# One-head cross-attention: queries from two fp16 parts, and rows turned by a SyncE transfer

## The chip, the cores and the metric

The kernel runs on one core of one Trainium2 chip. The metric is the device time of one execution in microseconds (us); the median of the runs shown is compared, lower is better.

## What is computed

A decoder of two layers on 2048 rows of width 256, with a context of 1601 rows of width 192. Layer 0: self-attention with 16 heads, cross-attention with 16 heads, a mixture of 8 experts (top 2). Layer 1: linear attention with a short convolution, **cross-attention with one head**, and a product quantised to fp8. The change is in the one-head cross-attention, whose reference is, on layer-normed rows:

```python
query = image_features @ Wq + bq
key = text_features @ Wk + bk
value = text_features @ Wv + bv
scores = query @ key.T / sqrt(256)
weights = softmax(scores, axis=-1)
attended = weights @ value            # added to the rows x
```

## The kernel before, in words

`cross_one_head` (L2338 to L2706) works on 16 tiles of 128 rows (T = 16). The two weight matrices Wq and Wk are folded into one matrix `fold` before the stage, so that a query of 192 (padded to 256) columns meets the context itself; `near` is its bias, `side` the share of the bias in a row's sum. Each engine has its own instruction stream, written out by hand; semaphores order them. For tile n:

- GpSimd (L2384 to L2394) normalises the rows into `oxn` (L2390) and multiplies them by `side` into `oprods` (L2394). L2390 of tile n waits until TensorE has turned tile n-2, L2394 until VectorE has summed the previous product.
- TensorE turns the rows in two transposes (`turn_x`, L2421) into the bank `ops_x`; ScalarE copies them to `oxt` (`copy_x`, L2524); TensorE makes the query with four fp32 products against `fold` (`query`, L2428; the trace shows two instructions for each). ScalarE evicts it with its bias as the high fp16 part `oqh` (L2531), VectorE makes the low part `oql` (L2598).
- `score`: each of four blocks of up to 512 keys gets five fp16 products (L2441 to L2445) into the four banks `ops_s`.
- VectorE takes the maximum of the first 1024 keys (`front`, L2609) and of the other 577 (`maximum`, L2614), and makes the bias `onm` of the exponential (L2621). ScalarE takes the exponentials of both parts into `opn` with their sums (`weights`, L2539).
- ScalarE casts them to fp16 as the high part `oph` (`high`, L2546, in two pieces), VectorE makes the low part `opl` (`low`, L2627, in two pieces). SyncE turns each with one transposing transfer (L2405, L2409).
- `values`: 13 blocks of three fp16 products (L2459 to L2461) against the context rows into the bank `ops_o`. The other half of this bank takes the turned attention (`turn_o`, L2470) and its product with Wv (`project`, L2476), which VectorE adds to the rows (`add`, L2642). `values(n)` waits for `add(n-1)` (semaphore "o"). In between ScalarE scales and evicts the attention (`evict`, L2553) and copies it turned (`copy_o`, L2559).

The tiles overlap. In its iteration n TensorE does: score(n+1) block 0, turn_x(n+2), turn_o(n-2), score(n+1) block 1, project(n-2), score(n+1) blocks 2 and 3, query(n+2), values(n-1). ScalarE: evict(n-2), high(n, 0), copy_x(n+2), copy_o(n-2), high(n, 1), query(n+2), weights(n+1). VectorE: low(n, 0), low(n, 1), front(n+1), add(n-2), maximum(n+1), low part of query(n+2), share(n) (the reciprocal of the sum), extremes(n-2), row_sum(n+3), and for n of 1 to 7 one step on the weights of the last stage. Before its loop TensorE does score(0), turn_x(1), query(1) and ten idle products that only keep it busy (`unused`, L113); VectorE does row_sum(0), row_sum(1), front(0), maximum(0), row_sum(2), and the low part of query(1). Tile 0's query is made in the stage before.

## Time and profile before

| | us |
|---|---|
| median of 3 runs | 1683.11 |
| lowest, highest | 1682.45, 1684.7 |
| the profiled execution, its own time | 1681.9 |
| its span, first to last instruction | 1680.1 |
| busy: TensorE (PE) | 1596.0 (95%) |
| busy: VectorE (DVE) | 1503.1 (89%) |
| busy: ScalarE (ACT) | 1318.8 (78%) |
| busy: GpSimd (POOL) | 395.6 (24%) |
| mean granted TensorE clock | 0.993 of 2.4 GHz |

The profile shows one execution. PEld is TensorE's loading of weights, which runs beside its products; SPq is SyncE's queue, whose rows show the issue of a transfer. A row of the timeline gives start and duration of one instruction (or of several of one line, with their count), and in brackets how long its engine had been idle and what released it. Products are pipelined: each shows some 0.2 us more than its distance to the next. The stage of the change runs from about 1488 to 1646 us of the span.

### The profile page before, as it was taken

What the parts mean: (1) busy time and instruction counts of PE and PEld (TensorE: products, weight loads), DVE (VectorE), ACT (ScalarE), POOL (GpSimd) and SP (SyncE); (2) the same over time, 40 slices, a digit from 0 to 9 for tenths busy, and PEclk for the clock granted to TensorE, in tenths of its full rate; (3) what the DMA queues carried; (4) which work ended last, traced back from release to release, by engine and by line L of the source; (5) the groups of instructions that cost most, each with busy time, mean ns of one, the idle gap of its engine ahead of it and who ended that gap; (6) DMA issues with size and microseconds to landing.
All of it is one profiled execution on the core that took longest, in us unless ns stands there. A gap on an engine that the chain in (4) does not pass through costs nothing. (4 is left out here: it accounts for less than half of the span.)

```text
span 1680.1 us, 36592 instructions
## 1 busy us (share of the span) xinstructions
PE 1596.0 (95%) x14452; PEld 631.1 (38%) x14452; DVE 1503.1 (89%) x2190; ACT 1318.8 (78%) x2590; POOL 395.6 (24%) x658
## 2 busy tenths in 40 slices
PE   6999999999999999999999999999989999789997
PEld 3542222232223232223322222222235555657773
DVE  6899999989999999989899999999948887788867
ACT  4619999879898989898899999999985565545644
POOL 5800010212123312312211111111013443533300
PEclk9999999999999999999999999999999999999998
DMA  4001001001101200111221011010001000025551
GB/s 147 14 7 20 14 14 14 14 14 26 27 14 24 42 14 14 33 20 24 70 55 26 14 21 20 14 27 14 14 30 60 1 1 1 1 37 96 94 103 51
DMA packets 148027, 52.34 MB, mean 31 GB/s; under 512 B 137424, under 2 KB 146128, under 8 KB 147600
## 3 DMA queue, kind: packets, MB, share of 16 engines
q1 hardware_dynamic: 147152, 48.62, 14.1%
q8 instruction: 115, 1.88, 0.5%
q10 hardware_dynamic: 704, 1.38, 0.2%
q14 instruction: 56, 0.46, 0.1%
HBM read 14.07 MB, written 2.10 MB: 10 GB/s over the span
## 5 line engine op out<-in xcount | busy, mean ns | idle before, releaser
L968 DVE TENSOR_REDUCE mxp<-ps_m 128x2 f32<-128x1024 f32 (+2 forms) x928 | 1048.8, 1195 | 41.5 <-PE ps_m L747 40.1
L897 ACT ACTIVATE work<-ps_s 128x512 f32<-128x512 f32 x1856 | 1001.7, 598 | 76.5 <-PE ps_s L771 48.9
L797 PE MATMUL ps_av<-work,vst 128*32 128x256 f32 x7424 | 592.8, 391 | 14.7 <-ACT avs L904 12.3
L771 PE MATMUL ps_s<-qb,k_stack 50*128 50x512 f16 x1856 | 565.8, 382 | 0.5 <-ACT v_rows L915 0.3
L747 PE MATMUL ps_m<-k_stack,qa 48*128 48x512 f16 (+1 forms) x2048 | 534.5, 358 | 2.3 <-PEq L1123 0.5
L797 PEld LDWEIGHTS ps_av<-work,vst 128*32 128x32 f32 x7424 | 147.1, 108 | 383.1 <-ACT work L897 321.6
L771 PEld LDWEIGHTS ps_s<-qb,k_stack 50*128 50x128 f16 x1856 | 119.6, 94 | 378.6 <-ACT work L897 322.9
L747 PEld LDWEIGHTS ps_m<-k_stack,qa 48*128 48x128 f16 x2048 | 108.3, 93 | 21.5 <-DVE mxp L968 14.8
L616 POOL TENSOR_SCALAR mtmp<-negm 128x16 f32<-128x16 f32 x32 | 8.2, 255 | 390.3 <-DVE negm L973 390.2
L602 POOL COPY vst<-v_rows 128x1024 f32<-128x1024 f32 (+1 forms) x32 | 30.6, 956 | 144.4 <-PE ps_av L797 144.3
L682 POOL TENSOR_TENSOR q_rows<-avs,rc 128x256 f32<-128x256 f32 x31 | 19.2, 619 | 173.2 <-DVE rc L979 173.2
L1603 PE MATMUL pbank<-k_stack,pxh 128*128 128x512 f16 x128 | 48.7, 380 | 5.8 <-ACT pscaled L1752 3.3
L2627 DVE TENSOR_TENSOR opl<-opn,oph 128x1024 f16<-128x1024 f32 (+1 forms) x32 | 32.2, 1041 | 21.9 <-ACT oph L2546 17.7
L2459 PE MATMUL ops_o<-k_stack,opht 128*128 128x192 f16 (+1 forms) x195 | 48.0, 246 | 1.7 <-DVE x_res L2642 1.7
L1604 PE MATMUL pbank<-k_stack,pxh 128*128 128x512 f16 x128 | 48.5, 379 | 0.0
L2461 PE MATMUL ops_o<-k_stack,oplt 128*128 128x192 f16 (+1 forms) x195 | 47.9, 246 | 0.0
L2460 PE MATMUL ops_o<-rows_l,opht 128*128 128x192 f16 (+1 forms) x195 | 47.9, 246 | 0.0
L1106 POOL CAST qnat<-q_rows 128x256 f16<-128x256 f32 x60 | 22.2, 398 | 97.9 <-issue 51.2
L2531 ACT ACTIVATE oqh<-ops_x,near 128x128 f16<-128x128 f32 x30 | 9.4, 364 | 42.4 <-PE ops_x L2428 42.4
L1607 PE MATMUL pbank<-k_stack,pxl 128*128 128x512 f16 x128 | 38.1, 379 | 0.0
L1752 ACT ACTIVATE pscaled<-pbank,pmix 128x256 f32<-128x256 f32 x64 | 26.6, 465 | 13.7 <-PE pbank L1607 7.0
L2539 ACT ACTIVATE opn<-ops_s,onm 128x1024 f32<-128x1024 f32 (+1 forms) x32 | 29.4, 924 | 9.8 <-DVE onm L2621 9.5
(442 smaller groups left out, 1993.6 us busy)
## 6 DMA issues: line engine op xcount, KB each, us to landing
x_res<-in_x SPq DMA_DIRECT2D x4, 512.0 KB, 8.1
w_experts<-in_w_experts SPq DMA_DIRECT2D x1, 2048.0 KB, 8.1
out<-x_res SPq DMA_DIRECT2D x8, 256.0 KB, 2.1
v_rows<-in_ctx_c SPq DMA_DIRECT2D x1, 1664.0 KB, 7.1
work<-in_ctx_t SPq DMA_DIRECT2D x1, 1456.0 KB, 15.3
ctx_n<-in_ctx_n SPq DMA_DIRECT2D x1, 1248.0 KB, 7.6
w_qkv<-in_w_qkv ACTq DMA_DIRECT2D x1, 768.0 KB, 8.5
w_qkv<-in_w_qkv SPq DMA_DIRECT2D x1, 768.0 KB, 4.2
```

The costliest lines, as they stand in the source:

```text
L747: m = pe.matmul(ps_m[:, b, e, col:col + width], qa[n % 3][e * HALF:e * HALF + MAXROWS, a, j, :], STACKS[g][e * HALF:e * HALF + MAXROWS, gr ...
L771: pe.matmul(ps_s[:, bank, :], STACKS[part(n)][rows, group(n) * PAIRS + j, t * P:t * P + P], qb[n % 2][rows, :, j, :], start=True, stop=Tru ...
L797: m = pe.matmul(ps_av[32 * h:32 * h + 32, cols], vst[n % 2][:, t, h, :], pbuf[(tau[n] + t) % 2][:, h, cols], start=(t == 0 and half == 0), ...
L897: a.activation(pbuf[g % 2][:, h, :], ps_s[:, b, :], ACT.Exp, scale=factor).then_inc(s["exp"], 1)
L968: v.tensor_reduce(dst, src, AX.X, ALU.max).then_inc(s["mred"], 1)
L1603: pe.matmul(bank[i % 2][:, :], xh[n % 2][:, k, :], weh[:, k, cols], start=(k == 0), stop=False)
L1604: pe.matmul(bank[i % 2][:, :], xh[n % 2][:, k, :], wel[:, k, cols], start=False, stop=False)
L1607: m = pe.matmul(bank[i % 2][:, :], xl[n % 2][:, k, :], weh[:, k, cols], start=False, stop=(k == 1))
L2459: pe.matmul(att(n), pht[n % 2][0:r, t, :], vh[0:r, t, :], start=(t == 0), stop=False)
L2460: pe.matmul(att(n), pht[n % 2][0:r, t, :], vl[0:r, t, :], start=False, stop=False)
L2461: m = pe.matmul(att(n), plt[n % 2][0:r, t, :], vh[0:r, t, :], start=False, stop=(t == TM - 1))
L2627: v.tensor_tensor(pl[:, PIECES[k]], pn[n % 2][:, PIECES[k]], ph[:, PIECES[k]], ALU.subtract).then_inc(s["pl"], 1)
```

## The change

The rows and the folded weights are split into two fp16 parts each, and the query is the sum of three products of parts (high-high, high-low, low-high) in place of the fp32 product, twelve fp16 products per tile in place of four fp32 ones. The rows' parts (`xs`, 128 x 512 in fp16) are turned by one transposing transfer on SyncE's queue in place of TensorE's two transposes and ScalarE's copy. ScalarE makes the high part of the rows (`high_row`) and, once, of the weights (`fs`); GpSimd makes the low parts (`low_row`, and once for the weights). The order of GpSimd's work and the places of the new steps are in the diff. The sequence of VectorE is unchanged.

```diff
--- before.py
+++ after.py
@@ -2339,7 +2339,7 @@
 
 
     nc = prog["nc"]
-    s = {k: fresh(prog, "x" + k) for k in ("norm", "var", "root", "rstd", "xn", "xtr", "xcp", "qm", "qh", "ql", "sc", "mx", "nm", "ex", "ph", "pl", "hi", "lo",
+    s = {k: fresh(prog, "x" + k) for k in ("norm", "var", "root", "rstd", "xn", "xh", "xl", "x_in", "fp", "qm", "qh", "ql", "sc", "mx", "nm", "ex", "ph", "pl", "hi", "lo",
                                            "av", "o", "o2", "r", "rr", "oe", "otr", "ocp", "y", "pad", "sh", "neg", "sca", "top", "wf")}
     FRONT = 1024
     LAST = M - (TM - 1) * P
@@ -2349,7 +2349,9 @@
     with ExitStack() as cx:
         def sb(name, shape, dt=F32):
             return cx.enter_context(nc.sbuf_tensor(name, shape, dt))
-        xn, xt = [first[0], sb("oxn1", [P, D])], [first[1], sb("oxt1", [P, 2, P])]
+        xn = [first[0], sb("oxn1", [P, D])]
+        xs, xt = ([sb(f"o{k}{p}", [P, *shape], F16) for p in range(2)] for k, shape in (("xs", (2, D)), ("xturned", (4, P))))
+        fs = sb("ofs", [P, 2, 2, D], F16)
         qh, ql = ([first[i], sb(f"o{k}1", [P, 2, P], F16)] for i, k in ((2, "qh"), (3, "ql")))
         pn = [sb(f"opn{p}", [P, MP]) for p in range(2)]
         ph, pl = (sb(f"o{k}", [P, MP], F16) for k in ("ph", "pl"))
@@ -2381,9 +2383,13 @@
                 g.memset(oc[p][:, C + 1:D], 0.0).then_inc(s["pad"], 1)
             for rows in (ph, pl):
                 g.memset(rows[:, M:MP], 0.0).then_inc(s["pad"], 1)
+            def low_row(n):
+                g.wait_ge(s["xh"], n)
+                g.tensor_tensor(xs[n % 2][:, 1, :], xn[n % 2][:, :], xs[n % 2][:, 0, :], ALU.subtract).then_inc(s["xl"], 1)
+
             for n in range(T):
-                if n >= 2:
-                    g.wait_ge(s["xtr"], n - 1)
+                if n >= 3:
+                    g.wait_ge(s["xl"], n - 2)
                 if n == FIRST_T:
                     g.wait_ge(s["rstd"], 1)
                 if n > 0:
@@ -2392,11 +2398,28 @@
                 g.wait_ge(s["xn"], n + 1)
                 g.wait_ge(s["r"], 2 * n)
                 g.tensor_tensor(prods[:, :], xn[n % 2][:, :], side[:, 0:D], ALU.mult).then_inc(s["r"], 1)
+                if n == 0:
+                    g.wait_ge(s["fp"], 1)
+                    g.tensor_tensor(fs[:, 1, :, :], fold[:, :, :], fs[:, 0, :, :], ALU.subtract).then_inc(s["fp"], 1)
+                if n > 0:
+                    low_row(n)
 
         @block.sync
         def _(e):
+            def turn_x(n):
+                e.wait_ge(s["xh"], n)
+                e.wait_ge(s["xl"], n)
+                if n >= 3:
+                    e.wait_ge(s["qm"], n - 1)
+                if n > 1:
+                    e.wait_ge(s["x_in"], 16 * (n - 1))
+                e.dma_start_transpose(xt[n % 2][:, :, :], xs[n % 2][:, :, :].rearrange("p s d -> p (s d)")).then_inc(s["x_in"], 16)
+
+            turn_x(1)
             e.wait_ge(s["pad"], 7)
             for n in range(T):
+                if n + 2 < T:
+                    turn_x(n + 2)
                 e.wait_ge(s["ph"], 2 * n + 2)
                 if n > 0:
                     e.wait_ge(s["hi"], 16 * n)
@@ -2413,20 +2436,16 @@
 
         @block.tensor
         def _(pe):
-            def turn_x(n):
-                pe.wait_ge(s["xn"], n + 1)
-                if n > 0:
-                    pe.wait_ge(s["ql"], n)
-                for k in range(2):
-                    m = pe.transpose(ps_x[:, k, :], xn[n % 2][:, k * P:k * P + P], ident[:, :])
-                m.then_inc(s["xtr"], 1)
-
             def query(n):
-                pe.wait_ge(s["xcp"], n + 1)
+                pe.wait_ge(s["x_in"], 16 * n)
+                pe.wait_ge(s["ql"], n)
+                if n == 1:
+                    pe.wait_ge(s["fp"], 2)
                 for c in range(2):
                     for k in range(2):
-                        m = pe.matmul(ps_x[:, 2 + c, :], fold[:, k, c * P:c * P + P], xt[n % 2][:, k, :],
-                                      start=(k == 0), stop=(k == 1))
+                        for i, j in ((0, 0), (0, 1), (1, 0)):
+                            m = pe.matmul(ps_x[:, 2 + c, :], fs[:, i, k, c * P:c * P + P], xt[n % 2][:, 2 * j + k, :],
+                                          start=((k, i, j) == (0, 0, 0)), stop=((k, i, j) == (1, 1, 0)))
                 m.then_inc(s["qm"], 1)
 
             def score(n, b):
@@ -2479,18 +2498,14 @@
             def unused(count):
                 idle_products(pe, ps_i[:, :], kh[:, 0, 0:P], kh[:, 0, 0:512], count)
 
-            pe.sem_inc(s["xtr"], 1)
             pe.sem_inc(s["qm"], 1)
             for b in range(4):
                 score(0, b)
-            turn_x(1)
             query(1)
             unused(10)
             for n in range(T):
                 if n + 1 < T:
                     score(n + 1, 0)
-                if n + 2 < T:
-                    turn_x(n + 2)
                 if n >= 2:
                     turn_o(n - 2)
                 if n + 1 < T:
@@ -2519,9 +2534,11 @@
             back = a.alloc_register("one_undo")
             a.reg_load(back, undo[0:1, 0:1].bitcast(I32))
 
-            def copy_x(n):
-                a.wait_ge(s["xtr"], n + 1)
-                a.copy(xt[n % 2][:, :, :], ps_x[:, 0:2, :]).then_inc(s["xcp"], 1)
+            def high_row(n):
+                a.wait_ge(s["xn"], n + 1)
+                if n >= 3:
+                    a.wait_ge(s["x_in"], 16 * (n - 2))
+                a.copy(xs[n % 2][:, 0, :], xn[n % 2][:, :]).then_inc(s["xh"], 1)
 
             def query(n):
                 a.wait_ge(s["qm"], n + 1)
@@ -2558,24 +2575,25 @@
                     a.wait_ge(s["y"], n)
                 a.copy(oct[:, :, :], att_t).then_inc(s["ocp"], 1)
 
-            a.sem_inc(s["xcp"], 1)
             a.sem_inc(s["qh"], 2)
+            a.copy(fs[:, 0, :, :], fold[:, :, :]).then_inc(s["fp"], 1)
             a.wait_ge(s["var"], 1)
             a.activation(tmp[:, 0, FIRST_T:T], tmp[:, 1, FIRST_T:T], ACT.Sqrt).then_inc(s["root"], 1)
             a.wait_ge(s["pad"], 7)
             a.activation(warm[:, :], warm[:, :], ACT.Exp)
-            copy_x(1)
+            high_row(1)
             weights(0)
+            high_row(2)
             query(1)
             for n in range(T):
                 if n >= 2:
                     evict(n - 2)
                 high(n, 0)
-                if n + 2 < T:
-                    copy_x(n + 2)
                 if n >= 2:
                     copy_o(n - 2)
                 high(n, 1)
+                if n + 3 < T:
+                    high_row(n + 3)
                 if n + 2 < T:
                     query(n + 2)
                 if n + 1 < T:
```

## Rows read from the trace of the kernel before

**Rows 1.** Busy time: stretch, us; PE, PEld, DVE, ACT, POOL (count); clock, DMA share, GB/s

```profile
1541.09:1550.00 8.91, 8.91 (x77) 7.03 (x75) 7.62 (x19) 5.07 (x12) 3.03 (x3) 1.00 0.52 98
1621.08:1629.70 8.62, 6.87 (x60) 5.14 (x58) 6.21 (x16) 4.17 (x9) 0.00 (x0) 1.00 0.53 99
```

**Rows 2.** Timeline, middle tile: start us, us, engine, line, operation

```profile
1541.02 2.26 POOL L2390 TENSOR_SCALAR oxn<-x_res,ln_mean,ln_rstd 128x256 f32<-128x256 f32 x1 [0.46 <-PE ops_x L2421]
1541.09 2.13 DVE L2627 TENSOR_TENSOR opl<-opn,oph 128x1024 f16<-128x1024 f32 x2 [1.12 <-issue]
...
1543.78 1.91 SPq L2409 DMA_TRANSPOSE oplt<-opl  x1
...
1544.14 1.14 PE L2428 MATMUL ops_x<-oxt,fold 128*128 128x128 f32 x8
...
1544.58 0.41 DVE L2642 TENSOR_TENSOR x_res<-ops_o,x_res 128x256 f32<-128x256 f32 x1
...
1545.14 0.24 PE L2459 MATMUL ops_o<-k_stack,opht 128*128 128x192 f16 x1
...
1548.56 0.42 ACT L2553 ACTIVATE ooc<-ops_o,orr 128x192 f32<-128x192 f32 x1 [0.38 <-PE ops_o L2461]
...
1549.44 0.38 PE L2421 MATMUL ops_x<-ident,oxn 128*128 128x128 f32 x2
...
1549.66 0.38 PE L2470 MATMUL ops_o<-ident,ooc 128*128 128x128 f32 x2
...
1550.00 2.13 DVE L2627 TENSOR_TENSOR opl<-opn,oph 128x1024 f16<-128x1024 f32 x2 [1.11 <-ACT oph L2546]
```

**Rows 3.** Timeline of the last full tile, TensorE and VectorE

```profile
1624.89 0.24 PE L2459 MATMUL ops_o<-k_stack,opht 128*128 128x192 f16 x1 [0.77 <-DVE x_res L2642]
...
1629.70 1.90 DVE L2627 TENSOR_TENSOR opl<-opn,oph 128x1024 f16<-128x1024 f32 x2 [2.23 <-ACT oph L2546]
```

**Rows 4.** Timeline of VectorE: first maxima of the fourth and last tile

```profile
1516.73 1.22 DVE L2609 TENSOR_REDUCE omx<-ops_s 128x1 f32<-128x1024 f32 x1
...
1623.20 1.21 DVE L2609 TENSOR_REDUCE omx<-ops_s 128x1 f32<-128x1024 f32 x1
```

**Rows 5.** Timeline of TensorE, first stage: eight fp16 products and what follows

```profile
34.31 0.62 PE L1183 MATMUL hkps<-identh,hknat 128*128 128x128 f16 x8
34.77 0.39 PE L1161 MATMUL hturn<-ident,hxn 128*128 128x128 f32 x2
```

**Rows 6.** Groups (count; busy us, mean ns), and one DMA issue (us to landing)

```profile
L1300 ACT CAST qnat<-q_rows 128x256 f16<-128x256 f32 x4 | 1.6, 403 | 0.0
...
L1107 POOL TENSOR_TENSOR qnat<-q_rows,qnat 128x256 f16<-128x256 f32 x30 | 20.1, 671 | 2.4
...
qa<-qnat SPq DMA_TRANSPOSE x32, 3.0
```

**Rows 7.** Timeline of the stage's start, VectorE and TensorE

```profile
1491.28 0.42 DVE L2593 TENSOR_REDUCE occ<-oprods 128x1 f32<-128x256 f32 x1 [1.17 <-POOL oprods L2394]
...
1493.61 2.32 PE L113 MATMUL ops_i<-k_stack 128*128 128x512 f16 x10
...
1497.63 0.39 PE L2441 MATMUL ops_s<-k_stack,oqh 128*128 128x512 f16 x1 [1.70 <-DVE oql L2598]
...
1501.11 1.22 DVE L2609 TENSOR_REDUCE omx<-ops_s 128x1 f32<-128x1024 f32 x1
```

**Rows 8.** Busy time of TensorE: stretch, us; PE busy; clock, DMA share, GB/s

```profile
24.06:26.47 2.41, 0.00 (x0) 1.00 0.00 0
26.80:30.00 3.20, 3.20 (x5) 0.50 0.01 3
```

**Rows 9.** Timeline of the first stage: VectorE beside GpSimd

```profile
33.84 0.41 DVE L1327 TENSOR_TENSOR hknat<-k_rows,hknat 128x256 f16<-128x256 f32 x1
...
57.33 0.96 POOL L1433 TENSOR_TENSOR k_rows<-k_rows,shift 128x256 f32<-128x256 f32 x1
...
57.63 0.95 DVE L1327 TENSOR_TENSOR hknat<-k_rows,hknat 128x256 f16<-128x256 f32 x1
```

## The prediction

> **What bounds the kernel now.** I read the page's share of busy time first: TensorE is busy for 95% of the span. The change touches only the one-head attention, some 150 us of it, so I went to the busy time by stretch and to the timeline of one tile there. In a tile in the middle TensorE is busy for all of its 8.91 us, while VectorE has 7.62 and ScalarE 5.07 [rows 1]. That looks like a stage bound by TensorE alone. The last full tile, the only one in which TensorE makes no query and turns no rows, says otherwise: TensorE is busy for 6.87 us there, and the tile still takes 8.62 [rows 1]. So I looked for a second cycle of the same length, in the waits of that tile and in the timeline of the middle one.
>
> There is one, and it runs through a PSUM bank. The product of the weights with the values (`values`, L2459) writes the bank in which the output of an earlier tile stands until VectorE has added it to the rows (L2642), so `values` waits for `add`. In the middle tile [rows 2]: `add` starts at 1544.58, `values` at 1545.14 (0.56: 0.41 of `add` and 0.15 to be seen); ScalarE's eviction at 1548.56 (3.42); the cast of the high parts and then VectorE's low parts (L2627) at 1550.00 (1.44); the next `add` follows the start of the low parts by 1544.58 - 1541.09 = 3.49. Sum: 0.56 + 3.42 + 1.44 + 3.49 = 8.91, the whole tile. The query before `values` starts at 1544.14, so it fills its time up to 1545.14 and the wait is invisible. In the tile without a query it is seen: `values` stands idle for 0.77 us on x_res of L2642 [rows 3]. **Both** cycles are thus as long as the tile, and shortening one uncovers the other. From the fourth tile's maximum to the last one's, 12 tiles take 1623.20 - 1516.73 = 106.47, or 8.87 each [rows 4].
>
> **What leaves TensorE.** A pair of turns of one tile takes 0.22 (1549.44 to the next work at 1549.66), and its query of four fp32 products, eight instructions, 1.00 (1544.14 to 1545.14) [rows 2]. In their place come twelve fp16 products with 128 columns. Eight instructions of that shape and type take 34.77 - 34.31 = 0.46, so 0.058 each [rows 5], and twelve 0.69. TensorE saves 0.22 + 1.00 - 0.69 = 0.53 per tile, over the 13 steady tiles 6.9 us. TensorE's own cycle falls to about 8.4.
>
> **What that is worth.** The cycle through `add` contains neither the query nor the turn. Its length without them is measured in the last full tile: 8.62 [rows 1, 3]. The difference to 8.91 is mostly the low parts, 2.13 us for the pair in the middle and 1.90 in the last tile [rows 2, 3]: in the middle GpSimd's normalisation of the next rows starts 0.07 before them and contends. The change moves this normalisation: it no longer waits for TensorE's turn but follows GpSimd's new subtraction, which waits for the cast that ScalarE makes after the second high part. So it leaves the low parts' window, and I take 8.62 for all 12 tiles: 12 x 8.62 = 103.4, a gain of 3.0, and 0.2 more for the low parts one tile earlier. **Steady part: -3.2 us**, against -6.9 by TensorE's account. Bounds: nothing gained if the low parts stay at 2.13, up to -6.9.
>
> **What is added and is covered.** ScalarE: the copy out of PSUM goes (it was behind the first high part, not on the cycle), and a cast of 0.40 [rows 6] comes behind the second one, where ScalarE waits for the query anyway. GpSimd: a subtraction of 0.67 per tile [rows 6]; it has 3.03 busy in 8.91 [rows 1]. SyncE's queue gets a third transpose per tile between the low part's and the next high part's. The low part's issue starts at 1543.78 and holds SyncE for 1.91 [rows 2]; the new one follows and has some 5 us until the next high part. What it waits for (both parts, the query two tiles back, its predecessor) is older than that. A transpose of 1024 columns lands in 3.0 [rows 6]; this one has 512, and I take 3.0 (bounds 1.5 and 4.0). TensorE wants it almost a tile later, so it costs nothing in the steady part. If the cover went, it would be this landing.
>
> **The start is not covered.** Tile 1's query is the first of the stage. Before, TensorE turned and multiplied it at once, ran ten idle products from 1493.61 (2.32), and began tile 1's scores at 1497.63, released by VectorE's low part of the query [rows 7]. Now three things come ahead:
> - On GpSimd the low part of the folded weights (512 columns, twice 0.67 = 1.3) goes ahead of the rows and products of tile 1. VectorE's row sum of tile 1 already waits for that product (idle 1.17 before 1491.28) [rows 7], and the first maximum stands behind it in VectorE's order. So tile 0's exponentials move by 1.3, and the second cast adds 0.4 before the query's eviction: scores of tile 1 no earlier than 1497.63 + 1.7 = 1499.3.
> - The rows: product of tile 1 done at 1491.25 + 1.3, subtraction to 1493.3, landing at 1496.3. TensorE has nothing to do from about 1491.9, for 4.4 us.
> - The clock. In the first stage TensorE idled from 24.06 to 26.47 and was then granted 0.50 of 2.4 GHz, the 1.2 GHz level, through 30.00, some 3.6 us after it had restarted [rows 8]. An idle 4.4 us should do the same. From 1496.3 the query takes 1.4 at half speed, five of the ten idle products (still in front of the scores) take 0.43 each up to 1500.0, the rest 0.215 each (ten in 2.32 with the drain of the last): scores from about 1501.0.
>
> The tile's first maximum follows two blocks of scores, 2.15 and 0.3 later, so at 1503.4 instead of 1501.11 [rows 7]: **start +2.2 us** (with the clock kept: 1501.8, +0.7; with a slower landing and clock: +5).
>
> **Sum:** -3.2 + 2.2 = -1.0. Against the profiled execution's own 1681.9 that is 1680.9. That execution lies 1.2 under the median of the runs, so I put the change on the median: 1683.1 - 1.0 = **1682.1**. A measurement of this kernel can tell about 0.2%, 3.4 us; this is under it.
>
> **Rivals.** *TensorE was the only bound.* For it: 8.91 of 8.91 busy. Against it: the 0.77 of waiting in the tile without a query. It would give -6.9 + 2.2 = -4.7, with the clock kept -6.2: 1677 to 1678.5.
>
> *GpSimd's new subtraction blocks VectorE's low parts (slower).* By my times the subtraction becomes ready about 0.1 us after the second low part has started, too close to call. The trace has such a meeting: a subtraction of VectorE that started at 57.63, inside a GpSimd operation of 57.33 to 58.29, took 0.95; the same one at 33.84 took 0.41 [rows 9]. If GpSimd comes first, each of 13 tiles pays 0.54 (the subtraction's own 0.67 at most) on the cycle through `add`: 7.0, in all +6.0, so 1689. It decides as soon as the subtraction starts before the second low part, that is, if the cast is 0.1 earlier than I think. Against it: the normalisation that started first in the middle tile cost the low parts only 0.23 [rows 2, 3]. On this the Trainium skill (SBUF — State Buffer, the two sides and their ports) says that the shared port pair is an exclusive lock and that the loser fully blocks for the whole instruction of the other. By that rule the outcome is whoever starts first, 0 or 0.67 per tile; the trace agrees in rows 9, and not in the 0.23 of rows 2.
>
> *The start costs more.* A landing of 4 us or a longer stretch at 1.2 GHz gives +5 there: 1685.
>
> **Chances.** Forecast with its own range (1679.5 to 1684) 0.54; blocked low parts 0.22 (fully, or part of the tiles); TensorE the only bound 0.13; dear start 0.11. The range reaches from 1678 to 1689 and leaves out the better half of the gain and the worst of the blocking. Faster by over 0.2% (under 1679.7): the third case and a little of the first, 0.17. Slower by over 0.2% (over 1686.5): most of the blocking and a little of the dear start, 0.24. Between: 0.59.
>
> **What would show it.** Right: a middle tile of 8.6 to 8.7; `values` with about 0.3 idle before it, released by L2642 in nearly every tile; low parts at 1.90 for the pair; a granted clock of 0.50 after 1494 in the start; the first scores of tile 1 some 3 us later against the stage's begin. Wrong: tiles of 8.4 without idle time before `values` (TensorE alone); a second low part of 1.2 and more, with GpSimd's subtraction inside it (blocking); TensorE waiting for the turned rows in a middle tile (the transfer is not hidden).

## The result, and the profile after

The changed kernel takes 1686.63 us (median of 22 runs, 1684.39 to 1688.2), the kernel before, on the same chips, 1684.43 (22 runs, 1682.45 to 1686.26). The ratio is 1.0013, with a 95% interval of 1.0008 to 1.0019: slower by 0.13%, 2.2 us. The forecast was 1682.1, 1.0 us faster than the 1683.1 then known for the kernel before; over more runs that kernel is at 1684.43. The result lies in the forecast's range and within the 0.2% called "the same", but on the other side: slower, and not faster.

The profiled execution took 1688.2 us, its span is 1686.4. Everything below is measured from the first GpSimd memset of this stage, here called the **begin** (1488.01 before, 1491.37 after). In sixteen more profiles it lies between 1488.3 and 1492.0, with the same code ahead of it, so 3.4 us of the difference between the two profiles are none of the change's. From the begin to the end of the span it is 192.1 us before and 195.0 after: + 2.9.

From the page of the changed kernel (engines; the instruction queue of the DMA; the group of `values`, with busy time, mean ns, idle time and what ended it):

```profile
PE 1596.4 (95%) x14479; PEld 627.1 (37%) x14482; DVE 1503.9 (89%) x2190; ACT 1319.6 (78%) x2591; POOL 400.6 (24%) x674
...
q8 instruction: 115, 1.88, 0.4%
...
L2478 PE MATMUL ops_o<-k_stack,opht 128*128 128x192 f16 (+1 forms) x195 | 47.9, 246 | 3.6 <-DVE x_res L2660 3.1
```

TensorE makes its queries faster, and is still busy for 95%. The group of `values` now shows 3.6 us of idle time, 3.1 of it released by the `add` (L2660). The page of before had 1.7 there. What the query gave up turns into this wait.

**A steady tile.** Timeline of a middle tile of the changed kernel (the subtraction of the low rows is L2388), and its busy time (columns as in [rows 1]), which answer to [rows 1, 2]:

```profile
1546.91 1.90 DVE L2645 TENSOR_TENSOR opl<-opn,oph 128x1024 f16<-128x1024 f32 x2 [1.11 <-issue]
...
1548.10 1.24 POOL L2388 TENSOR_TENSOR oxs<-oxn,oxs 128x256 f16<-128x256 f32 x1 [1.70 <-ACT oxs L2541]
...
1549.74 0.83 PE L2447 MATMUL ops_x<-oxturned,ofs 128*128 128x128 f16 x12
1550.17 0.41 DVE L2660 TENSOR_TENSOR x_res<-ops_o,x_res 128x256 f32<-128x256 f32 x1
...
1550.73 0.24 PE L2478 MATMUL ops_o<-k_stack,opht 128*128 128x192 f16 x1 [0.16 <-DVE x_res L2660]
```

```profile
1544.20:1552.87 8.67, 8.51 (x79) 6.52 (x78) 7.38 (x20) 5.09 (x13) 3.22 (x3) 1.00 0.60 113
```

VectorE's low parts take 1.90 for the pair, not 2.13. GpSimd's new subtraction (L2388) starts inside them and is the one that waits: 1.24 us instead of the 0.67 of [rows 6]. The query of twelve fp16 products takes 0.83 to its last drain. `values` at 1550.73 waits 0.16 for the `add` at 1550.17. The tile takes 8.67 (1552.87 - 1544.20), and TensorE is busy for 8.51 of it.

**Maxima.** Timeline of VectorE in the changed kernel, first maxima of tiles 1, 3 and 15, as in [rows 4, 7]:

```profile
1507.07 1.23 DVE L2627 TENSOR_REDUCE omx<-ops_s 128x1 f32<-128x1024 f32 x1 [1.48 <-PE ops_s L2464]
...
1523.01 1.22 DVE L2627 TENSOR_REDUCE omx<-ops_s 128x1 f32<-128x1024 f32 x1
...
1626.80 1.22 DVE L2627 TENSOR_REDUCE omx<-ops_s 128x1 f32<-128x1024 f32 x1
```

From tile 3 to tile 15 it is 1626.80 - 1523.01 = 103.79 for 12 tiles, against 106.47: **- 2.7 us**. But tile 1 comes 15.70 after the begin, where it came 13.10 after it [rows 7]: **+ 2.6 us**. Between tiles 1 and 3 another 0.3 is lost (15.94 against 15.62). At the maximum of tile 15 the two kernels are thus 0.2 us apart, 135.43 against 135.19.

**The start**, timeline of the changed kernel and busy time by stretch; they answer to [rows 7, 8]:

```profile
1496.87 6.61 SPq L2416 DMA_TRANSPOSE oxturned<-oxs  x2
...
1499.32 1.46 PE L2447 MATMUL ops_x<-oxturned,ofs 128*128 128x128 f16 x12 [4.15 <-DMA oxturned<-oxs]
...
1500.57 4.31 PE L113 MATMUL ops_i<-k_stack 128*128 128x512 f16 x10
...
1504.71 0.38 PE L2460 MATMUL ops_s<-k_stack,oqh 128*128 128x512 f16 x1
```

```profile
1495.17:1499.32 4.15, 0.01 (x1) 0.01 (x1) 3.41 (x9) 1.02 (x4) 3.16 (x4) 0.81 0.16 32
1499.32:1504.71 5.39, 5.39 (x22) 2.76 (x23) 2.71 (x5) 4.44 (x10) 3.18 (x4) 0.51 0.13 26
1504.71:1507.10 2.39, 2.39 (x13) 1.09 (x12) 0.88 (x4) 0.00 (x0) 2.30 (x2) 1.00 1.07 200
```

TensorE idles 4.15 us for the turned rows, and from its restart at 1499.32 it is granted about half the clock for 5.4 us, the level of 1.2 GHz. All ten idle products run at it: 4.31 us instead of 2.32.

**The tail.** After tile 15's maximum there are 56.9 us left before and 59.6 after, **+ 2.7**, in code that the change hardly touches. Before, `values` of tile 15 started and ran like this (timeline of TensorE, then busy time):

```profile
1636.50 0.24 PE L2459 MATMUL ops_x<-k_stack,opht 128*128 128x192 f16 x1 [1.05 <-DMA oplt<-opl]
```

```profile
1636.50:1639.70 3.20, 3.20 (x39) 3.19 (x40) 0.00 (x0) 0.37 (x1) 0.00 (x0) 1.00 0.02 5
```

and in the changed kernel:

```profile
1641.17 0.32 PE L2478 MATMUL ops_x<-k_stack,opht 128*128 128x192 f16 x1 [2.12 <-DMA oplt<-opl]
```

```profile
1641.17:1644.40 3.23, 3.23 (x20) 3.06 (x21) 0.00 (x0) 0.00 (x0) 0.00 (x0) 0.50 0.00 0
1644.40:1646.40 2.00, 2.00 (x24) 1.97 (x22) 0.00 (x0) 0.37 (x1) 0.00 (x0) 0.97 0.00 0
```

TensorE waits 2.12 us for the last low transpose instead of 1.05. Then it is granted 0.50, and the values take from 1641.17 to 1646.05, 4.9 us, where they took 3.3. (The end is taken here and in the table below at the start of the last product but one; the last drains 0.32 us later in every kernel.) These two items, 1.1 and 1.6, are the whole of the 2.7 in this profile. The second is not the same in every execution; the part on the tail comes back to it.

### The profile page after: what moved, and what is told of

The parts are those of the page before. It is cut to its first block and busy times, and to the rows that moved or that the text cites. A ratio compares the mean times of both kernels' runs of the same rounds, so it can differ in the third digit from the quotient of the medians.

```text
span 1686.4 us, 36720 instructions
## 1 busy us (share of the span) xinstructions
PE 1596.4 (95%) x14479; PEld 627.1 (37%) x14482; DVE 1503.9 (89%) x2190; ACT 1319.6 (78%) x2591; POOL 400.6 (24%) x674
## 3 DMA queue, kind: packets, MB, share of 16 engines
q8 instruction: 115, 1.88, 0.4%
```

## Experiments

Sixteen runs were made, of fourteen new kernels and, for a second profile, of the changed kernel (after_2) and of one combination (best_2). One table for all: median and ratio to the kernel before (95% interval), and from the one profile of each: the first maximum after the begin, the 14 steps to tile 15's maximum, the landing of the last low transpose, the end of tile 15's values after its maximum, and the time from the begin to the end.

| kernel | median us | ratio | tile 1 | 14 steps | landing | values end | begin to end |
|---|---|---|---|---|---|---|---|
| before | 1684.43 | 1 | 13.10 | 122.09 | 4.2 | 16.57 | 192.1 |
| changed | 1686.63 | 1.0013 (1.0008-1.0019) | 15.70 | 119.73 | 5.3 | 19.25 | 195.0 |
| after_2 | 1686.50 | 1.0014 (1.0006-1.0023) | 15.83 | 119.72 | 5.4 | 19.37 | 195.2 |
| start_old | 1685.35 | 1.0001 (0.9992-1.0010) | 12.75 | 121.29 | 5.5 | 17.86 | 192.3 |
| start_v2 | 1683.83 | 1.0001 (0.9992-1.0010) | 14.14 | 119.72 | 5.3 | 17.66 | 191.9 |
| idle_first | 1682.85 | 0.9989 (0.9980-0.9998) | 14.17 | 119.62 | 5.5 | 17.76 | 191.9 |
| order | 1682.50 | 0.9995 (0.9986-1.0004) | 14.02 | 119.73 | 5.3 | 19.16 | 193.3 |
| calm | 1686.18 | 1.0011 (1.0002-1.0020) | 15.87 | 119.52 | 5.4 | 19.38 | 195.2 |
| own_before | 1683.36 | 0.9992 (0.9984-1.0001) | 13.12 | 121.97 | 4.3 | 16.13 | 191.6 |
| own_after | 1681.96 | 0.9986 (0.9977-0.9994) | 15.80 | 117.19 | 5.4 | 17.24 | 190.6 |
| pad4 | 1683.76 | 0.9999 (0.9990-1.0008) | 15.80 | 119.77 | 4.3 | 16.58 | 192.5 |
| pad12 | 1690.59 | 1.0035 (1.0021-1.0048) | 14.81 | 124.00 | 5.5 | 17.77 | 196.9 |
| shift | 1683.78 | 0.9998 (0.9989-1.0007) | 14.16 | 119.62 | 4.3 | 17.02 | 191.2 |
| tail_idle | 1685.03 | 1.0007 (0.9998-1.0016) | 15.78 | 119.72 | 5.3 | 17.59 | 193.5 |
| order_shift | 1682.45 | 0.9988 (0.9979-0.9998) | 12.97 | 119.60 | 4.3 | 16.60 | 189.5 |
| own_order | 1676.94 | 0.9963 (0.9951-0.9975) | 14.28 | 115.96 | 4.2 | 16.06 | 186.6 |
| best | 1681.96 | 0.9986 (0.9977-0.9995) | 13.54 | 115.87 | 4.3 | 17.16 | 186.9 |
| best_2 | 1681.69 | 0.9984 (0.9975-0.9993) | 15.38 | 116.94 | 4.2 | 17.15 | 189.8 |

The ratio compares each kernel with the kernel before in its own batch, whose median went from 1683.6 to 1684.6. So medians of two batches can differ by about 1 us without a cause in the kernels, and the ratios are the safer comparison. Most rows rest on 11 or 12 executions, pad12 on 5 and own_order on 6.

### The start

**start_old**: tile 1's query made the old way. Two more things moved with it: ScalarE's cast for tile 2 went behind tile 0's high part, and the low part of the folded weights went behind tile 1's product on GpSimd (not shown below).

```diff
-            query(1)
+            (two fp32 turns into ps_x, ScalarE's copy, fp32 products with fold)
             unused(10)
...
             weights(0)
-            high_row(2)
...
+                if n == 0:
+                    high_row(2)
```

> The changed kernel, with tile 1's query made as before (two fp32 turns, ScalarE's copy, four fp32 products), and with the low part of the folded weights behind tile 1's product on GpSimd; all other tiles stay as changed. Theory (the steady tiles gain what the cycle through add leaves, about 3.0 us; the start loses 3.2): reduce of tile 1 about 13.1 us after the stage's begin as in the kernel before, middle tiles 8.6 to 8.7, so 2.5 to 3 us faster than the kernel before. Rival (the steady tiles gain nothing on other executions, and what is seen between two profiles is the clock): within 1 us of the kernel before. Rival (TensorE the only bound, the loss all in the start): 6 to 7 us faster.

Tile 1 came 3 us earlier, at 12.75, but the next step took 9.65 us instead of 8.08: I had put the cast for tile 2 too late, so that its transfer and the query waited. At tile 15's maximum 1.4 of the 3 us were left. A flaw of my edit, mended in **start_v2** (the cast where the changed kernel has it, GpSimd's order as in start_old):

> The changed kernel with tile 1's query alone made the old way (two fp32 turns and a copy, then fp32 products); high_row(2) stands where the changed kernel has it, behind the weights of tile 0, which the first try at the old start had too late. Theory (the start costs 2.6 us, because TensorE idles for the SyncE turn, drops to half its clock and then does ten idle products slowly): first maximum at 12.8 to 13.3 us after the stage's first GpSimd memset (15.7 in the changed kernel, 13.1 before), step from tile 1's to tile 2's maximum 7.9 to 8.3, and 2.5 us less than the changed kernel in all: 1684.1 against 1686.6, within 0.1% of the kernel before. Rival (the start's loss is made up later, since the steady part is set elsewhere): first maximum as early, but the 15th maximum at 135.2 as before and no gain in the total. The last low transpose should still land after 5.3 us, if the instruction fetch meets it.

The steps are the changed kernel's, 119.72, and the median is 1683.83, 2.8 under it. But tile 1's maximum is at 14.14, not the 12.8 to 13.3 expected: TensorE idled 2.36 us in front of the scores of tile 1, and the first seven ran at half speed (0.61 to 0.63 us each, 0.38 at full). The loss is therefore partly the clock's and not the transfer's. From the begin to the end start_v2 is 3.1 us under the changed kernel, and 1.6 of these lie in the tail, where its clock fell earlier and under cover (see the tail).

**idle_first**: nineteen idle products in front of tile 1's query, none behind it.

```diff
-            query(1)
-            unused(10)
+            unused(19)
+            query(1)
```

> The changed kernel with nineteen idle products ahead of tile 1's query in place of ten behind it. Theory (TensorE waits 4.2 us for the first transfer, its clock falls to 1.2 GHz, and the ten idle products then take 4.3 us in front of the scores): the clock stays at 1.00, the scores of tile 1 begin about 2 us earlier, released by VectorE's low part of the query, and the kernel is 1.5 to 2 us faster than the changed one, about equal to the kernel before. Rival (the start is bound by VectorE's later first maximum, and the clock is covered): less than 0.5 us faster than the changed one.

The clock stays at full speed, the idle time in front of the query falls to 0.56 on its weight load, the query takes 0.84 instead of 1.46. Tile 1's maximum is at 14.17, **1.5 us earlier** with the same transfer. The steps are unchanged, 119.62. So of the 2.6 us at the start 1.5 are the clock's. The kernel gained more than the 1.5 to 2 expected: 3.1 us from the begin to the end and 3.8 in the median. Half of that lies in the tail, which the idle products were not meant for.

**order**: the folded low part behind tile 1's rows on GpSimd.

```diff
-                if n == 0:
-                    g.wait_ge(s["fp"], 1)
-                    g.tensor_tensor(fs[:, 1, :, :], ...)
                 if n > 0:
                     low_row(n)
+                if n == 1:
+                    g.wait_ge(s["fp"], 1)
+                    g.tensor_tensor(fs[:, 1, :, :], ...)
```

> The changed kernel with the folded weights' low part (1.16 us on GpSimd) behind the rows' work of tile 1 instead of in front of it. Theory (GpSimd's order at the start sets when tile 0's exponentials, tile 1's transfer and the first query come): the transfer is issued 1.2 us earlier, TensorE's idle time in front of the first query falls from 4.15 to 3.0 or less, and the first maximum comes 1.0 to 1.2 us earlier; total - 1.0 against the changed kernel, 1685.5. Rival (the query then waits for the low part instead, so nothing is gained): the first maximum as before. Where TensorE's clock does not fall in the shorter gap, the gain at the maximum is up to 2.2 us.

TensorE's idle time before the query is 3.34 us, not 4.15, the query is at full speed, but the ten idle products still take 4.01 us. The transfer is issued 0.8 earlier after the begin, and tile 1's maximum comes at 14.02, 1.7 earlier; the rest is the faster query and the few products at full speed. The median is 4.1 under the changed kernel's, about 3.0 by the ratios, and 1.7 from the begin to the end; the profiled execution (1685.27) is one of the slower four of eleven, with the clock fallen in the tail, so what the faster seven did is not seen.

What the order alone is worth is seen between two kernels of the next parts, both with the clock at full speed at the start: **shift**, with the order of the changed kernel, has tile 1's maximum at 14.16, and **order_shift**, with the order of this run, at 12.97. That is 1.2 us, and 12.97 is even earlier than the 13.10 of the kernel before. In the changed kernel tile 0's maximum already comes 5.04 us after the begin instead of 3.92, with this order 3.93. The 2.6 us at the start are thus 1.5 of clock and about 1.1 of GpSimd's low part of the folded weights (1.16 us) standing in front. With both mended, nothing of the loss is left for the transfer itself.

### The steady part

**own_before, own_after**: the values' product in a bank of its own, so that it doesn't wait for the `add`.

```diff
+        ps_v = cx.enter_context(nc.psum_tensor("ops_v", [P, 512], F32))
...
-            return ps_o[:, 0:C] if n < T - 1 else ...
+            return ps_v[:, 0:C] if n < T - 1 else ...
...
-                        pe.wait_ge(s["o"], n)
+                        pe.wait_ge(s["oe"], n)
```

> The kernel before with the same separate bank. Theory (there TensorE has no idle time: both cycles are 8.9): the tile goes from 8.91 to 8.88 only, the time stays within 0.5 us. Rival (add was the true bound of the kernel before and TensorE had slack): 8.7 a tile, 2 to 3 us faster.

> The changed kernel with the product of weights and values in a PSUM bank of its own, so that it waits for the eviction of the tile before and no longer for add. Theory (in the changed kernel values waits for add, TensorE is idle 0.3 us a tile): the tile falls from 8.65 to TensorE's own 8.37, over 12 to 13 tiles 3.3 us, so 1 to 1.5 us faster than the kernel before and 3.3 faster than the changed one. Rival (the tile is bound by VectorE and ScalarE alone, or by GpSimd's share of the port): the tile stays at 8.6 to 8.7 and the time within 1 us of the changed one.

With the cycle through `add` cut, the old kernel's tiles stay at 8.88: TensorE has that much work. The changed kernel's fall to 8.13 to 8.37 in nine of the last twelve, and to 8.36 at the end, so its TensorE has about 8.4. Both cycles are there, as read: before, 8.9 and 8.62; after, 8.4 and 8.62. Three tiles took 9.26, 8.74 and 8.76. There the low parts took 2.37, 2.45 and 2.46; ahead of the first of them VectorE had waited for a low transpose that landed after 6.3 us, where most take 4.2 to 4.4. The forecast's blocking rival is real, for three tiles. That the late landing is what shifted VectorE against GpSimd was read from this one trace and not tested. From the begin to the end own_after is 4.4 us under the changed kernel, more than the 3.3 expected: 2.5 lie in the steps, 2.0 in the tail.

**pad4, pad12**: four or twelve products into the idle bank behind each query from tile 3 on.

```diff
                 m.then_inc(s["qm"], 1)
+                if n > 2:
+                    for _ in range(4):     # 12
+                        pe.matmul(ps_i[:, 0:P], kh[:, 0, 0:P], kh[:, 0, 0:P], start=True, stop=True)
```

> Four products of 128 fp16 columns into the idle bank behind each query from tile 3 on (13 tiles): about 0.23 us more TensorE work per tile; their results are read by nobody. Theory (a steady tile of 8.62 is set by a cycle through the add that frees the shared bank, with TensorE waiting 0.15 to 0.3 per tile in front of the values): the steps stay at 8.62 to 8.7 and the wait shrinks to 0.0 to 0.1, total + 0 to + 0.5 us over the changed kernel. Rival (TensorE alone is the bound, the wait is one that another would replace): 13 x 0.23 = + 3.0 us, steps 8.85. Beside that, 52 more TensorE instructions move its instruction fetches; if one of them made the last low transpose land late, that landing may go back from 5.3 to about 4.2, worth - 1.1 us, and up to - 2.7 with the clock fall behind it.

> The same with twelve products, 0.69 us per tile. Both theories have TensorE as the bound by then. Cycle theory: 0.15 to 0.3 of it goes into the wait, so the steps grow by 0.4 to 0.55, 13 x 0.45 = + 5.9 us over the changed kernel. Rival: 13 x 0.69 = + 9.0 us. The last landing may move by 1.1 us either way as in the run with four.

Groups of `values` on TensorE in tiles 1 to 14, in the changed kernel, with four and with twelve products (the last number is the idle time that the `add` ended):

```profile
L2478 PE MATMUL ops_o<-k_stack,opht 128*128 128x192 f16 (+1 forms) x176 | 43.3, 246 | 2.6 <-DVE x_res L2660 2.1
```

```profile
L2481 PE MATMUL ops_o<-k_stack,opht 128*128 128x192 f16 (+1 forms) x178 | 43.8, 246 | 1.0 <-DVE x_res L2663 1.0
```

```profile
L2481 PE MATMUL ops_o<-k_stack,opht 128*128 128x192 f16 (+1 forms) x169 | 41.6, 246 | 0.0
```

The wait shrinks from 2.6 to 1.0 and to 0.0. With four products the steps are as long as without (119.77): 0.23 us of TensorE's work per tile is free. With twelve a tile takes 9.03, + 0.35 to + 0.41, where they are 0.67 of work (9.03 - 8.36 of the own bank). In the median pad12 is 4.0 over the changed kernel, not the 5.9 expected; its steps cost 4.3, and 1.5 came back in the tail. The forecast's cycle is the bound after the change, with 0.3 us of room in TensorE. pad4 also brought **- 2.9 us** on the changed kernel in the median (2.4 by the ratios), nearly all of it in the tail (2.7 by the profile; next part).

**calm**: the cast for tile n+3 behind the query's evictions.

```diff
-                if n + 3 < T:
-                    high_row(n + 3)
                 if n + 2 < T:
                     query(n + 2)
+                if n + 3 < T:
+                    high_row(n + 3)
```

> The changed kernel with ScalarE's cast for tile n+3 moved from in front of the query's evictions to behind them, so that GpSimd's subtraction (0.67 us) no longer runs beside VectorE's two subtractions of 1024 and 641 columns. Theory (two engines that both read two operands from the local memory wait for one another; where GpSimd is first VectorE's pair takes 2.4 us for 1.9, where VectorE is first GpSimd takes 1.2 us for 0.67): the pair takes 1.90 in tiles 0 and 1 as well, the step from tile 1's to tile 2's maximum is 7.5 instead of 8.08, steady steps stay 8.62 (there GpSimd is the one that waits), and 0.5 to 1.0 us less than the changed kernel's 1686.6. Rival (the long pair of the first tiles comes from the low clock or the first use of the code, not from GpSimd): 2.4 as before and no gain. The late last landing (5.3 us) stays in either case, since TensorE's instructions are the same.

VectorE's low parts of tiles 0 and 1 with GpSimd's products of tile 0 beside them, timeline of the changed kernel:

```profile
1502.86 2.42 DVE L2645 TENSOR_TENSOR opl<-opn,oph 128x1024 f16<-128x1024 f32 x2 [0.32 <-ACT oph L2563]
...
1503.40 1.26 POOL L2400 TENSOR_TENSOR oprods<-oxn,side 128x256 f32<-128x256 f32 x1
...
1512.55 2.38 DVE L2645 TENSOR_TENSOR opl<-opn,oph 128x1024 f16<-128x1024 f32 x2 [1.47 <-ACT oph L2563]
```

and of calm:

```profile
1500.74 2.43 DVE L2645 TENSOR_TENSOR opl<-opn,oph 128x1024 f16<-128x1024 f32 x2 [0.32 <-ACT oph L2563]
...
1501.28 1.27 POOL L2400 TENSOR_TENSOR oprods<-oxn,side 128x256 f32<-128x256 f32 x1
...
1510.73 1.90 DVE L2645 TENSOR_TENSOR opl<-opn,oph 128x1024 f16<-128x1024 f32 x2 [1.26 <-ACT oph L2563]
```

Tile 1's pair is at 1.90 again, so there it was GpSimd's subtraction. Tile 0's is not: there GpSimd's product of rows (L2400) starts 0.54 us after the first part, waits for its end, gets in between the two parts and takes 1.26 instead of 0.73. Most of what the one pair gave is gone again: the step is 7.74 instead of 8.08 and the next one 8.00 instead of 7.86, 0.2 in all. Neither the median nor the time from begin to end changes. The low parts of the first tiles are not what sets the time there.

### The tail

**shift**: 64 narrow products in front of tile 1's query, 130 us ahead of the tail.

```diff
+            for _ in range(64):
+                pe.matmul(ps_i[:, 0:32], kh[:, 0, 0:P], kh[:, 0, 0:32], start=True, stop=True)
             query(1)
             unused(10)
```

> 64 products of 32 columns (whose results nobody reads) go in front of tile 1's query, in TensorE's idle time at the start; all the rest is the changed kernel. They move TensorE's fetches of instructions against its work. Theory (in the changed kernel a fetch happens to run while the last low transpose is under way, which then lands after 5.3 instead of 4.2 us; TensorE waits 2.1 instead of 1.05 us for it and its clock falls to half for the last values): no fetch within the last transposes, low(15) lands after 4.2 to 4.4, the values of tile 15 start 13.4 us after its maximum instead of 14.5, and the clock stays at 1.00; 1.1 to 2.7 us less than the changed kernel, 1684 to 1685.5. If the 64 products also keep the clock up for the first query, the first maximum comes up to 1 us earlier as well. Rival (the late landing comes from the changed order of SyncE's transposes or of VectorE's writes): landing 5.3 and total unchanged.

The DMA view over the last two transposes, of three kernels with the same code there (40 equal slices of a stretch of 7 to 8 us: GB/s; the instruction queue, if it has a packet; us to landing). The changed kernel:

```profile
GB/s 0 0 0 0 0 0 143 218 215 209 210 213 218 222 180 159 209 250 279 123 36 0 1 8 9 10 9 176 290 290 290 288 142 0 0 0 0 0 0 0
...
q8 instruction: 1, 0.02, 0.7%
...
oplt<-opl SPq DMA_TRANSPOSE x1, 5.3
```

pad4:

```profile
GB/s 0 0 0 0 0 0 0 146 222 219 203 209 211 215 218 221 183 165 186 235 225 203 208 203 225 215 218 218 190 217 113 0 0 0 0 0 0 0 0 0
...
oplt<-opl SPq DMA_TRANSPOSE x1, 4.3
```

pad12:

```profile
GB/s 0 0 0 0 0 0 138 219 216 210 214 215 214 219 166 172 218 238 186 193 40 0 0 3 9 9 9 70 291 292 289 291 223 0 0 0 0 0 0 0
...
q8 instruction: 1, 0.02, 0.7%
...
oplt<-opl SPq DMA_TRANSPOSE x1, 5.5
```

**The instruction queue is the cause.** TensorE's instructions come over the same DMA engines, 16 KB at a time, 115 times in the execution (the page's q8 line: 1.88 MB), once in some 252 of its 28,961 records; that they are TensorE's is seen from what follows, since products of TensorE alone move them; pad12, with 156 more products and as many more weight loads, has 116. Where one meets the transposes, their stream of about 215 GB/s stops for some seven slices of 0.2 us, at 0 to 10 GB/s, and catches up at 290. Both landings are late: 5.5 and 5.3 instead of 3.9 and 4.3. In pad4 and shift, where 52 and 64 products ahead moved the fetches, none falls there and the landing is 4.3. (In shift the values still end at 17.02, 0.4 later than in pad4: the clock had fallen for part of tile 14's values, 0.37 us for one instead of 0.25. It kept its clock at the start instead, with tile 1 at 14.16.) In pad12, moved further by 104 products, one falls there again and it is 5.5. The kernel before has the same late landings in four tiles (5.4 to 5.9 at 1543.78, 1561.59, 1588.27 and 1606.03), where nearly a tile of slack hides them; in the last tile TensorE stands waiting.

The DMA view of every low transpose in all eighteen profiles says the same. Of 155 with no packet of this queue between issue and landing, none lands later than 4.5 us; of 133 with one, 109 land later than that, up to 6.3. The other 24 land after 3.9 to 4.5, so not every meeting costs.

**tail_idle**: eight idle products in TensorE's wait for that transpose.

```diff
+            unused(8)
             values(T - 1, range(0, 6))
```

> The changed kernel with eight products into the idle bank (1.7 us) in TensorE's wait for the last low transpose, in front of tile 15's values. Theory (the wait of 2.1 us for a transfer that an instruction fetch delays lets the clock fall to half for the last values, 4.8 instead of 3.2 us): landing unchanged at 5.3, values of tile 15 start 14.5 us after its maximum as before, but they end at 17.7 instead of 19.2; total - 1.0 to - 1.6 against the changed kernel, 1685.0 to 1685.6. Rival (the clock falls for another reason, for instance because it has been granted for too long before): the values still take 4.8 in the slow profiles and the total is unchanged.

Timeline of TensorE:

```profile
1638.32 1.89 PE L113 MATMUL ops_i<-k_stack 128*128 128x512 f16 x8
1640.55 0.24 PE L2478 MATMUL ops_x<-k_stack,opht 128*128 128x192 f16 x1 [0.34 <-DMA oplt<-opl]
```

The transfer is as late, the values end at 17.59 instead of 19.25, and the median is 1.5 lower than that of after_2, 1.2 by the ratios. The granted clock over the whole execution is 0.993 in ten of its eleven runs and 0.992 in the other, in those of after_2 it is 0.991 or 0.992. So without the fall the second item, 1.6 us, is gone.

**Where the clock falls is less certain than where the transfer lands.** Busy time of idle_first in tile 14's values and in tile 15's, and of start_old in tile 15's, whose first row on TensorE stands behind it:

```profile
1631.80:1634.30 2.50, 2.50 (x18) 2.37 (x16) 0.63 (x2) 0.00 (x0) 0.00 (x0) 0.50 1.61 140
1636.70:1639.90 3.20, 3.20 (x39) 3.19 (x40) 0.00 (x0) 0.37 (x1) 0.00 (x0) 1.00 0.00 0
```

```profile
1640.63:1643.83 3.20, 3.20 (x39) 3.19 (x40) 0.00 (x0) 0.37 (x1) 0.00 (x0) 1.00 0.00 0
```

```profile
1640.63 0.24 PE L2482 MATMUL ops_x<-k_stack,opht 128*128 128x192 f16 x1 [2.34 <-DMA oplt<-opl]
```

In idle_first, start_v2, pad12 and shift the clock falls one tile earlier, in the values of tile 14, behind a wait of 0.95 us that the changed kernel has too and gets through at full speed. With a late landing this fall is free: TensorE would have waited for the transfer anyway (0.58 us are left of its wait in idle_first), and the last values run at full speed. start_old idles for 2.34 us in front of tile 15's values and keeps its clock, and so does own_before with 2.19; the changed kernel, after_2, order and calm idle for 2.1 to 2.2 and lose it. A late landing is thus worth 1.1 to 1.3 us by itself, and the 1.6 of clock come on top in four of the five profiles in which nothing filled the wait and the clock had not fallen before. What decides between them no run shows.

### What is left, and the combinations

**after_2**, the changed kernel again, and **best_2**, the combination again:

> The changed kernel, unaltered, for a second profile. Fixed by the program, if the theory holds: last low transpose landing after 5.3 to 5.4 us, TensorE's wait for it 2.1, values of tile 15 starting 14.5 us after its maximum, steps of 8.62 and 8.68. Free to vary: first maximum 14.1 to 15.9 us after the stage's first memset, last values 3.2 (clock kept) or 4.8 us (clock fallen). In all 1684.4 to 1688.2, median 1686.5. Rival (the late landing is a chance of one execution): landing 4.2 to 4.3 this time.

> The kernel of the combined run, unaltered, for a second profile. Its times reach from 1677.2 to 1683.3. Theory (executions differ by how often and where the clock falls, in stages ahead of this one as well): in a slow execution the stage's steps are the same 8.36 and the difference lies ahead of the stage's first memset (1488.3 in the first profile) and in single stretches at a clock of 0.5. Rival (transfers vary within the stage): single steps of 8.7 to 9.3 make the difference, and the stage begins at the same time.

after_2 repeats the changed kernel within 0.2 us from the begin to the end: landing 5.4, values ending at 19.37. The late landing belongs to the program. Its begin is at 1489.06, 2.3 us earlier than in the first profile, and its span shorter by 2.1: what differs between these two executions lies ahead of the stage.

**best**: own bank, order, tail_idle and calm, with twelve wide and 54 narrow products in front of tile 1's query and none behind.

```diff
+            unused(12)
+            for _ in range(54):
+                pe.matmul(ps_i[:, 0:32], kh[:, 0, 0:P], kh[:, 0, 0:32], start=True, stop=True)
             query(1)
-            unused(10)
```

> All that helped or should help, together: the values' own bank of PSUM, the folded low part behind tile 1's work, twelve wide and 54 narrow products in front of tile 1's query and none behind it, eight products in front of tile 15's values, and the cast for tile n+3 behind the query's evictions. By the single terms against the changed kernel (1686.6): own bank - 2.5 (8.36 instead of 8.62 for nine steps or more), start - 1.5 to - 2.6, no fetch in the last transposes and no clock fall there - 2.7: 1679 to 1680.5, which is 0.25 to 0.3% below the kernel before. Rival (the gains overlap, since the freed TensorE runs into transfers that come late instead, as three steps of 8.7 to 9.3 in the run with the own bank): 1681.5 to 1682.5.

Its two profiles, the stretch from the first scores of tile 1 on, best and then best_2 (busy time):

```profile
1499.20:1502.00 2.80, 2.80 (x13) 1.26 (x14) 2.51 (x5) 0.80 (x2) 0.64 (x1) 1.00 0.52 104
```

```profile
1500.00:1504.50 4.50, 4.50 (x11) 1.64 (x12) 2.44 (x5) 0.81 (x2) 0.67 (x1) 0.50 0.75 145
```

The same program idled 1.36 us in front of these scores both times; once the clock stayed, once it fell to 0.50, and tile 1's maximum came at 13.54 or 15.38. And an edit of mine cost 1.1: the eight idle products that helped with a late transfer stand in the way of a punctual one (values ending at 17.16, in own_order at 16.06). The run expected 1679 to 1680.5 and missed it; its rival, that gains overlap, named the time (1681.5 to 1682.5) but not this cause.

**order_shift, own_order**: only the order and the 64 narrow products; the same with the own bank.

> GpSimd's order of the run with the folded low part behind tile 1's work, and 64 narrow products in front of tile 1's query. If the two add up: first maximum 12.9 to 14.0 us after the first memset, last low landing 4.3, values of tile 15 at 13.4 after their maximum; against the changed kernel's 1686.6, - 1.2 to - 2.2 at the start and - 1.1 to - 2.7 in the tail: 1682 to 1683.5, below the kernel before by 0.05 to 0.15%. Rival (only one of them counts, because both only change where the clock falls): 1683.5 to 1684.5.

> The same with the values in a bank of PSUM of their own. If all adds up: a further - 2.5 us (steps of 8.36), 1679.5 to 1681. Rival (the faster steps move transfers and fetches so that some tiles wait, and the clock gives part of it back): 1681.5 to 1683, as with the own bank alone (1682.0).

order_shift: start 2.7 under the changed kernel, landing 4.3, values ending at 16.60; 189.5 from begin to end. The two remedies add up in the profile (- 5.5) and less in the median (- 4.1 against after_2). own_order is the fastest: **1676.94 us, ratio 0.9963 (0.9951 to 0.9975)**, 0.37% under the kernel before, and 9.6 us under after_2 in the median (8.5 by the ratios), from six runs. Its steps from tile 3 on are 8.19 to 8.37, the last low transpose lands after 4.2, and TensorE's wait for it is 0.48. Its time is better than the 1679.5 to 1681 expected; the term that was too small is not known.

best is 5 us slower in the median than own_order, though two of their profiles are only 0.3 apart from begin to end. These two are no fair pair: the profiled execution of best (1677.2) is its fastest of eleven, the one of own_order (1680.32) the second slowest of six. best_2's, nearer to the middle of its runs (1680.85), is 3.2 over own_order's. These 3.2 are 1.1 of filler in the tail, 1.1 of tile 1's later maximum in best_2, where the clock fell, and 1.0 in the 14 steps; what the other executions did, and so the rest of the 5, stays open.

## Why the prediction was wrong

**Right.** *What bounds the kernel.* The cycle through `add` and TensorE's own, both as long as a tile: shown by the own bank and by the padding. *The steady part.* Forecast - 3.2 with 8.62 for 12 tiles; measured 8.68 for six, 8.62 for the others, 103.79 in all: - 2.7. Why the six take 0.06 more was not looked into. *What is covered.* The third transpose lands after 2.4 to 2.9 in most tiles and after 4.2 to 4.3 in three, and TensorE never waits for it in a steady tile. *TensorE the only bound* (0.13) is refuted by pad4. *Blocked low parts* (0.22): GpSimd came second in the 11 tiles from 2 to 12 (1.19 to 1.28 instead of 0.67) and paid itself; the price of 0.54 was right (1.90 to 2.43), the place was not. That it came second was luck: the forecast had called the two starts too close to tell, and in the middle tile they are some 0.02 us apart (the pair starts at 1546.91, its second part some 1.17 later by its share of the columns, an estimate, the subtraction at 1548.10). The Trainium skill's lock (SBUF — State Buffer, section "SBUF: two separate sides") agrees with these rows better than I allowed: whoever starts first gets the shared ports for its whole instruction, and the other waits. The 0.23 of [rows 2] still does not follow it.

**Too small.** *The start*, + 2.2: query at 7.95 us after the begin (forecast 8.3), but TensorE was granted half the clock for 5.4 us after its restart, not for the 3.6 of [rows 8], so that all ten idle products were slow and not five. (From the forecast's own rows, 1503.4 and 1501.11, its term is + 2.3.) Tile 1's maximum: + 2.6. The 0.7 that the forecast gave for the start with the clock kept measured 1.1 (14.17 against 13.10 in idle_first). To this come + 0.6 in the step to tile 2 and - 0.3 in the next one; I had only the - 0.2. What sets the + 0.6 is open, since calm took the contention of one pair away and gained only 0.2.

**The step that failed** is a term that the sum did not have. It ended at the last steady tile, as if all that follows were the same; it was not: **+ 2.7 us in the tail**, 1.1 of a late transpose and 1.6 of clock behind it. With the start and the steady part as measured but nothing in the tail, the sum would be + 0.2; this term makes it + 2.9. I had read 8.62 off the last full tile, and the low part's price off a middle one, but not asked of the last tile, where TensorE already waited 1.05 for a transfer, what else could move. The trace of before had the sign: low transposes of equal size landing after 4.2 and after 5.9.

Sum by the profiles: + 2.6 + 0.3 - 2.7 + 2.7 = + 2.9, against + 2.2 in the medians. Without the late landing (pad4) the change is worth nothing either way: 0.9999 (0.9990 to 1.0008). So even then the forecast's - 1.0 is not there: the start and its neighbouring step ate the whole steady gain.

## What to carry to other kernels

A change in the number of TensorE's instructions moves its instruction fetches, and a fetch on an uncovered transpose cost 1.1 to 1.3 us here, and 2.7 with the clock; so read the tail by itself, and before judging an edit by 0.1% move the fetches with a few narrow products. Where TensorE waits for the first or last transfer of a stage, reckon with what a fallen clock costs behind the wait, as a bound and not as a certainty, and fill the wait with idle products only if the transfer is later than they are. A one-off preparation in front of a stage's first work is on its path too: GpSimd's 1.16 us cost 1.2. Two cycles of equal length have to be shortened together: the query alone gave 0.22 us a tile, the own bank alone 0.01, both 0.54.

## What the runs showed of the hardware

- TensorE's instruction fetch (16 KB) halts the transposes of SyncE's queue: 1.4 us at 0 to 10 GB/s between stretches of 215 and 290 (the changed kernel's last two). In all eighteen profiles no low transpose lands later than 4.5 us without such a fetch, and 109 of 133 do with one, up to 6.3.
- The same program, with the same idle time in front, got the full clock in one execution and 0.50 in another (best and best_2), and 2.36 us of idle time sufficed for a fall in start_v2, where 2.34 did not in the tail of start_old. The same wait of 0.95 us was followed by 0.50 in idle_first and by full speed in the changed kernel.
- A GpSimd operation with two operands that runs between VectorE's two low parts costs the pair 0.53 (1.90 to 2.43) and is itself stretched from 0.73 to 1.26; one that starts inside the second part is stretched from 0.67 to 1.24, and the pair stays at 1.90.
